# A two-layer recurrent and attention kernel: where ScalarE copies a batch's raw attention outputs

## The reference, cut to what matters

```python
scores = jnp.einsum('bhqd,bhkd->bhqk', q, k) * scale
scores = jnp.where(causal[None, None], -jnp.inf, scores)
attn = jax.nn.softmax(scores, axis=-1)
out = jnp.einsum('bhqk,bhkd->bhqd', attn, v)
out = out.transpose(0, 2, 1, 3).reshape(b, s, E)
s = out @ wo + bo
x = x + s * g
```

## Time and profile before

| | |
|---|---|
| median of 3 runs | 2126.52 us (2126.18 to 2131.17) |
| the profiled execution | 2133.49 us, its span 2131.8 us |
| mean granted clock of TensorE | 0.889 of full speed |
| busy over the span | PE 77%, DVE 75%, ACT 53%, POOL 48% |
| attention | from about 1722 us of the span to its end |

### The profile page before, as it was taken

The page is one execution under the profiler, slowest core; times in us unless marked ns, Lnnn a source line. Parts: engine busy times, 40 slices in busy tenths (PEclk is TensorE's granted clock), DMA queues, the critical chain, the costliest instruction groups (busy, mean ns, idle before and its releaser), DMA issues. The chain is left out here.

```text
span 2131.8 us, 32693 instructions
## 1 busy us (share of the span) xinstructions
PE 1652.0 (77%) x8418; PEld 1194.2 (56%) x8418; DVE 1599.4 (75%) x4329; ACT 1133.8 (53%) x1811; POOL 1024.1 (48%) x1108
## 2 busy tenths in 40 slices
PE   3286787886868868687785599998999988778877
PEld 2163454554535545354452488887888855555554
DVE  3499999999999999999998444444444466677663
ACT  1365465564746646456453345454454556666664
POOL 2577778687786867868887100000000013233322
PEclk8598788897988979889897699999999989999997
DMA  5420020110201102002002211110110000000000
GB/s 83 105 56 1 1 66 1 31 36 1 65 1 24 42 1 65 0 12 49 1 11 68 71 26 23 25 26 9 23 23 9 26 15 16 15 15 22 15 15 13
DMA packets 140707, 58.82 MB, mean 28 GB/s; under 512 B 94743, under 2 KB 135180, under 8 KB 140556
## 3 DMA queue, kind: packets, MB, share of 16 engines
q1 hardware_dynamic: 140556, 57.19, 12.0%
HBM read 36.05 MB, written 21.10 MB: 27 GB/s over the span
## 5 line engine op out<-in xcount | busy, mean ns | idle before, releaser
L612 ACT ACTIVATE shared_rings<-pb 128x512 f32<-128x512 f32 (+1 forms) x784 | 434.7, 598 | 361.1 <-PE pb L639 318.3
L688 PE MATMUL pb<-hid,shared_down 128*128 128x512 f32 x528 | 308.8, 670 | 156.7 <-POOL hid L490 154.0
L486 POOL TENSOR_TENSOR hid<-shared_rings 128x512 f32<-128x512 f32 x256 | 334.2, 1306 | 177.3 <-ACT shared_rings L612 162.5
L490 POOL TENSOR_TENSOR hid<-hid,shared_rings 128x512 f32<-128x512 f32 x256 | 329.9, 1289 | 20.6 <-POOL hid L486 1.0
L1814 DVE SCALAR_TENSOR_TENSOR l_acc<-l_pb,l_gtok,l_acc 128x128 f32<-128x128 f32 x512 | 144.3, 344 | 255.5 <-PE l_pb L1458 255.5
L637 PE MATMUL pb<-xt_hi,shared_hi 128*128 128x512 f32 (+1 forms) x264 | 191.9, 727 | 96.6 <-ACT shared_rings L612 96.6
L1373 ACT ACTIVATE l_hid<-l_pb,l_cols 128x512 f32<-128x512 f32 x256 | 169.3, 687 | 182.9 <-PE l_pb L1458 182.6
L1458 PEld LDWEIGHTS l_pb<-l_big,l_hid 128*128 128x128 f32 x2048 | 247.1, 192 | 10.6
L1458 PE MATMUL l_pb<-l_big,l_hid 128*128 128x128 f32 x2048 | 247.9, 275 | 0.0
L1287 POOL TENSOR_TENSOR l_ql<-l_rope,l_qh 128x512 f32 x8 | 10.3, 1284 | 459.1 <-ACT l_qh L1367 459.1
L688 PEld LDWEIGHTS pb<-hid,shared_down 128*128 128x128 f32 x528 | 102.6, 209 | 214.9 <-POOL hid L490 188.1
(11 more groups left out here) (319 smaller groups left out, 3821.5 us busy)
## 6 DMA issues: line engine op xcount, KB each, us to landing
z_scratch<-zs SPq DMA_DIRECT2D x128, 81.0 KB, 3.0
zr<-z_scratch SPq DMA_DIRECT2D x8, 1296.0 KB, 8.1
x_sb<-in_L_attn_x_dram SPq DMA_DIRECT2D x32, 64.0 KB, 2.0
shared_rings<-in_L_ffn_We_gate_dram SPq DMA_DIRECT2D x4, 512.0 KB, 5.7
shared_rings<-in_L_ffn_We_up_dram SPq DMA_DIRECT2D x4, 512.0 KB, 6.7
g_scratch<-zs SPq DMA_DIRECT2D x8, 256.0 KB, 2.8
y_scratch<-yo SPq DMA_DIRECT2D x8, 256.0 KB, 2.1
shared_down<-in_L_ffn_W_dram SPq DMA_DIRECT2D x4, 512.0 KB, 6.1
```

The lines of the kernel that those rows point to most:

```text
L486: pool.tensor_tensor(hid1[:, :], g, u, ALU.mult).then_inc(s_h1, 1)
L490: pool.tensor_tensor(hid[:, (p + par) % 2, :], hid1[:, :], c, ALU.mult).then_inc(s_h, 1)
L612: act.activation(dst, pb[0:n, what, :], ACT.Silu if what == 0 else ACT.Copy).then_inc(s_ev, 1)
L688: last = pe.matmul(pb[:, SUM, :], wd[0:n, p, :], hid[0:n, (p + par) % 2, :], start=(p == 0), stop=(p == PAIRS), skip_group_check=True)
```

## The change

ScalarE's raw copy of batch `bx` is issued at i = 17 of the step that computes its values, ahead of the copies of the next batch's transposed maxima, rather than at i = 0 of the following step, behind them. The copy, its size, its source and its target stay as they are, and so do the lists of all other engines. For the last batch there are no maxima in that step, so that its copy keeps its place in the order.

```diff
-        O_RAW, O_TB, O_NORM, O_OT, O_WO, O_END = 0, 1, 2, 4, 6, 7
+        RAW_AT, O_TB, O_NORM, O_OT, O_WO, O_END = 17, 1, 2, 4, 6, 7
...
+            def raw_out(b):
+
+                act.wait_ge(s_pv, (b + 1) * 4)
+                act.activation(o_raw, pb[:, 6:8, :], ACT.Copy).then_inc(s_raw, 1)
+
             def o_unit(b, i):
 
-                if i == O_RAW:
-                    act.wait_ge(s_pv, (b + 1) * 4)
-                    act.activation(o_raw, pb[:, 6:8, :], ACT.Copy).then_inc(s_raw, 1)
                 if i == O_WO:
...
                 for i in range(NU):
                     if bo is not None:
                         o_unit(bo, i)
+                    if bx is not None and i == RAW_AT:
+                        raw_out(bx)
                     if ba is not None:
                         a_unit(ba, pa, i)
```

## The result

The changed kernel took 2104.01 us in the median of four runs (2101.44 to 2104.40), the kernel before 2126.91 us in four runs (2126.18 to 2131.17). The ratio is 0.9872 with a 95% interval of 0.9854 to 0.9889. A second measurement on another chip gave 0.9868 (0.9851 to 0.9885). At the level of the kernel before that is 27 to 28 us less by the ratios and 22.9 us less by the medians of the first measurement, whose quotient, 0.9892, lies just outside the first interval. The forecast was 29.6 us less, 2097 us in a range of 2091 to 2112.

The account below looks back on a forecast made before the run. Batch boundaries bound it: TensorE idles 2.79 us for ScalarE's raw copy. Gains of 11 x 1.65 = 18.2 and 4 x (1.65 + 1.21) = 11.4 us, together 29.6, take 2126.5 to 2096.9 us; range 2091 to 2112.

Parts of the forecast that it names:

- The copy fits in front: ScalarE before the maxima: raw copy lies wholly in idle time, 0.38 us to spare, costed at nothing.
- TensorE's queue and k0's copy: Batch boundary: raw transposes follow k0, k1 waits for k0's copy; k1 at 1911.07 against 1912.41, 1.34 us gained.
- Inside the batch: Up to the third exponential: earlier q0 and outputs' transposes raise the gain, bounds 1.34 and 1.70, taken as 1.65 us.
- The clock: TensorE at the boundary: shorter idling lets the four slow batches regain 1.21 us each; other bound, none of it.
- Rival 1: TensorE's lower clock stays in as many batches as now; gain 24.8 us, time 2101.7; chance 0.18.
- two of the signs: Profile: no batch window with granted clock under 0.97; prediction wrong if the clock falls inside the batches.
- The tail: Fifteenth boundary, ahead of the last batch: counted like the ten full-clock batches, 1.65 us.
- Rival 2: TensorE's lower clock comes to every boundary; gain 11.5 us, time 2115.0; chance 0.08.
- rival 4: Score units: lower clock holds through them, 3.5 us in a batch, slower at 2151; chance 0.03.
- Rival 3: Within the batch: boundary's gain given back as another engine paces the step's end; gain 0, time 2126.5; chance 0.04.
- Rival 5: ScalarE at the boundary: copy is late and pushes the maxima; gain 6.3 us, time 2120.2; chance 0.04.

Follow-up runs that it names:

- doubled copy: Changed kernel with the raw copy done twice in a row, the second waiting for the first; ratio 0.9951 to the kernel before.
- late latents: Changed kernel with ScalarE's small copy of the latents issued at i = 11, off the boundary; ratio 0.9835, with a fill of nine idle matmuls 0.9825.
- maxima split: Changed kernel with the latents' copy at i = 11 and ScalarE's second copy of maxima behind k0's copy; ratio 0.9809, median 2093.46 us.

## Why the prediction was right, point by point

**The copy fits in front.** Right to a few hundredths: start after 0.92 us (0.93 forecast), 0.39 us to spare (0.38), maxima not moved. The doubled copy shows that the cover is no longer than that.

**TensorE's queue and k0's copy.** The wait that goes, the wait that comes and their order are as forecast: the transposes follow k0, and k1 waits for k0's copy (1.54 us against about 1.3). Moved one at a time, the transposes' place is worth 0.77 us a batch, and to take the raw copy out from between the maxima and k0's copy, with the transposes out of q0's way as well, the full 1.55. k1 starts 1.18 us earlier, not 1.34: k0's copy stands 0.44 us behind the start of the latents' copy (1874.72 - 1874.28), where I had taken the 0.30 us of the earlier trace rows. The trace of before held the right figure. At its boundary without a raw copy, where the latents' copy also follows the maxima, it is 0.44 us (1741.98 - 1741.54):

```profile
1741.54 0.42 ACT L1389 ACTIVATE l_big<-shared_down 33x256 f32<-33x256 f32 x1
1741.98 0.69 ACT L1393 ACTIVATE l_wqk<-l_pb,shared_rings 128x512 fp32r<-128x512 f32 x1
```

**Inside the batch.** The term was 1.65 us in bounds of 1.34 and 1.70, and it measured 1.55. The second step of it is seen in the rows: VectorE copies q0 2.34 us earlier (2.3 forecast), the outputs' transposes stand directly behind the second scores, and the third exponential waits 0.43 us rather than 0.80. Over 14 batches the term was 1.4 us too large, which the 0.14 us of the latents' copy more than covers.

**The clock.** This is the mis-sized term. I took the four slow batches as regained in full, 4.8 us, on the ground that no row showed a fall after 1.3 us of pause. In the profile after there were two longer distances, of 0.9 and 2.1 us, so that 2.0 us were regained; in the repeated one there was one of 0.9 us, and 4.1 were. The fall stands where no row of before had shown one, ahead of the second scores. Rival 1 was thus true in part, and two of the signs that the forecast named came about: windows of a batch under 0.97 (0.93 and 0.86), and a clock that falls inside the batches. That the longer distances are the clock's is shown by the windows and by the fills: in the kernel before, in the order with the copy behind k0's and with late latents, work put into the pauses takes away every longer distance of the fourteen. In the changed kernel itself the fill left one against one, so that for its own falls the part of the pause is argued and not shown. TensorE: Matmul & The Clock Gate of the Trainium skill (section "What's actually happening") says that activity releases the throttle; the trace agrees, 0.95 against 1.00 in granted clock over 290 us, with work that has no other use.

**The tail.** Counted as one more batch of 1.65 us, it gave 3.5 us in one profile and 1.7 in the other. Its first scores waited for ScalarE and VectorE's maxima as the code has it, and gained 1.4 us; the rest differs with the clock of the emptying steps.

**Where the total agrees by luck.** The profiled executions differ by 29.1 us against 29.6 forecast, but 2.0 of the 29.1 lie ahead of the first batch. The attention itself gave 27.1: 1.4 us less than forecast by the term inside the batch and 2.9 by the clock, against 1.8 more in the tail.

**The rivals.** Rival 2 (low clock everywhere) and rival 4 (through the score units) did not come: none of the fourteen distances after is longer than 24.15 us, and twelve are at the full clock's length. In the one of 24.15 us the lower clock did last into the third scores and beyond, for 2.1 us rather than the 3.5 of rival 4. Rival 3 (given back in the batch) falls, since what is gained at the boundary comes out in the distance of the batches: 0.43 of 0.44 us with late latents. Only with the maxima split as well does another wait cap it: k0 is copied 1.15 us earlier than with late latents alone, and the batch is 0.33 us shorter. Rival 5 (the copy late) did not come about, and the doubled copy gives its price: 0.54 us a batch at full clock for 0.57 us of delay.

**What stays open.** The ratio gives 27 to 28 us, the medians of the first four runs 22.9. The kernel before ran between 2123 and 2137 us on the chips used, 0.7%, where the forecast had taken 0.2% from its first runs. Much of that can lie ahead of the attention: in the thirteen profiles, which share all their code up to there, the first copy of v starts between 1729.5 and 1739.2 us. The size in us therefore rests on the distances of the profiles more than on the runs.

What decides whether a batch gets the lower clock stays open too. The length of the longest pause at the boundary doesn't order the kernels: 4 and 3 of 14 batches with 2.79 us (before, raw copy behind the maxima), 9 with 2.42 us, 8 with 2.31 us, 2 and 1 with 1.54 us, 6 with 1.51 us, 3 with 1.10 us.

## What to carry to other kernels

If an engine stands idle just before the instruction behind which another engine's queue is held, look for what can be moved into the idle time: the copy that was moved was free for as long as the gap (0.39 us left over), and 1.55 us a batch came back because both its consumer and the copy behind it moved up. Then ask at once what the freed engine waits for next: here k0's copy, and taking 0.44 us from in front of it gave 0.43 us a batch more. Judge two orders at the same clock before preferring one: two of these were equal at full clock and 0.5% apart in time, and with a fill the slower of them was level or ahead (0.9850 against 0.9871 for the other with its own fill, measured on another chip).

## What the runs showed of the hardware

TensorE's granted clock fell in long pauses, in short ones and inside work. In the kernel before the four falls lay in the pause of 2.79 us. With the raw copy behind k0's the nine falls lay 0.2 to 1.4 us behind the end of the pause of 2.4 us, in the matmuls. In the changed kernel, with 1.54 us of idling ahead of k1, it fell 1.7 to 1.9 us behind that pause, in the 0.66 us of idling ahead of the second scores; it did so in one or two batches of fourteen, and the others had the same timing. With late latents and split maxima it fell once in the fourteen, at the end, where no pause since the values had been longer than 0.74 us. Eleven idle matmuls in the pause of the changed kernel left 0.91 us of it and one fall.

Two copies on ScalarE can overlap by 0.1 us when they follow each other directly (the latents' copy started 0.92 us after a raw copy of 1.02 us), but not always: behind the maxima's copies it started 0.02 us after their end. k0's copy then started 0.30 or 0.31 us after the latents' copy in the first case and 0.44 or 0.45 us in the second, at every boundary of the kernel before and of the changed one where all three stages run, and also at the boundary of the kernel before that has no raw copy. Why the order in front makes this difference wasn't tried.
